# Deformable-convolution layer of a four-layer network: borders of its row tables written earlier, input restored in four pieces, bilinear samples summed two at a time in PSUM

## The reference

```python
# layer 0, position bias of its attention: a small MLP on every (query, key) offset
bias = sign(pos) * log1p(abs(pos))
bias = relu(bias @ cpb_w1 + cpb_b1)
bias = relu(bias @ cpb_w2 + cpb_b2)
bias = bias @ cpb_w3 + cpb_b3
# layer 1
d = conv1x1(depthwise3x3(x[:, :256]));  d = instance_norm(d)
off = conv3x3(d)                          # 18 offsets for each pixel
samples = bilinear(d, grid + off)         # 9 taps, 4 corners, weights (1-ly)(1-lx) ...
dc = einsum('bckhw,ock->bohw', samples, dc_w) + dc_b
dc = layer_norm_over_channels(dc)
das = d * sigmoid(dc)
g = sigmoid(dsc2(max(x[:, 256:])) + dsc2(mean(x[:, 256:])))
x = x * das + x * g
```

## Time and profile before

| | us |
|---|---|
| median of 3 runs | 4365.64 (4363.87 to 4365.74) |
| the profiled execution | 4366.62 |
| its span in the profile | 4364.8 |
| position bias, about | 156 to 2300 |
| layer 1, about | 2803 to 3519 |
| of it, first gather to last sample | 2952.6 to 3498.8 |

### The profile page before, as it was taken

One profiled execution on the slowest core, in us unless ns is written; L12 is line 12 of the kernel. 1 busy time (PEld: TensorE's weight loads), 2 busy tenths in 40 slices (PEclk: granted clock), 3 DMA queues, 4 the chain that ended last, 5 costly groups with the idle time before them and its releaser, 6 DMA issues. The chain is left out here.

```text
span 4364.8 us, 67125 instructions
## 1 busy us (share of the span) xinstructions
PE 3896.5 (89%) x18472; PEld 2384.1 (55%) x18472; DVE 2992.5 (69%) x4467; ACT 2579.8 (59%) x4583; POOL 2118.7 (49%) x1861
## 2 busy tenths in 40 slices
PE   2699999999999999999998999788888377969999
PEld 1455555555555555555556777547666242435553
DVE  7788888888888888888886333447888833235562
ACT  3599999999999999999994333222121330113331
POOL 1555555555555555555551555306667500026663
PEclk7799999999999999999999999889999677989999
DMA  1200000000000000000002000219999911353311
GB/s 45 98 9 11 10 9 9 11 10 9 11 9 9 9 11 10 9 10 10 10 9 81 0 0 0 69 51 350 371 387 376 341 46 60 137 140 69 69 40 77
DMA packets 146902, 326.59 MB, mean 75 GB/s; under 512 B 45737, under 2 KB 46761, under 8 KB 145789
## 3 DMA queue, kind: packets, MB, share of 16 engines
q1 hardware_dynamic: 105340, 174.46, 12.9%
q0 software_dynamic: 41472, 151.01, 8.9%
HBM read 246.14 MB, written 79.04 MB: 74 GB/s over the span
## 5 line engine op out<-in xcount | busy, mean ns | idle before, releaser
L502 POOL TENSOR_TENSOR cpb_sum<-cpb_tab 128x512 f32<-128x512 f32 x1028 | 1045.9, 1048 | 965.7 <-DVE cpb_r L632 965.4
L613 ACT ACTIVATE cpb_h<-cpb_z,net_vec 128x512 f32<-128x512 f32 x1536 | 1006.1, 697 | 50.7 <-PE cpb_z L553 38.2
L550 PE MATMUL cpb_z<-cpb_r,cpb_w2a 128*128 128x512 f32 x2048 | 858.6, 419 | 23.5 <-DVE cpb_h L673 23.5
L632 DVE SCALAR_TENSOR_TENSOR cpb_r<-cpb_sum,cpb_r 128x512 fp32r<-128x512 f32 x1024 | 695.4, 710 | 187.8 <-ACT cpb_r L607 187.8
L551 PE MATMUL cpb_z<-cpb_r,cpb_w2b 128*128 128x512 f32 x2048 | 801.3, 391 | 0.0
L553 PE MATMUL cpb_z<-cpb_r,cpb_w2a 128*128 128x512 f32 x2048 | 799.8, 391 | 0.0
L632 DVE SCALAR_TENSOR_TENSOR cpb_r<-cpb_z,cpb_r 128x512 fp32r<-128x512 f32 x1028 | 661.8, 685 | 160.3 <-ACT cpb_r L607 154.6
L607 ACT ACTIVATE cpb_r<-cpb_z 128x512 fp32r<-128x512 f32 x1028 | 560.4, 604 | 139.5 <-PE cpb_z L537 139.5
L607 ACT ACTIVATE cpb_r<-cpb_sum 128x512 fp32r<-128x512 f32 x1024 | 598.5, 648 | 2.0 <-POOL cpb_sum L502 2.0
L550 PEld LDWEIGHTS cpb_z<-cpb_r,cpb_w2a 128*128 128x128 f32 x2048 | 384.0, 187 | 365.9 <-issue 301.0
L1480 DVE SCALAR_TENSOR_TENSOR dc_acc<-dc_g,dc_wt,dc_acc 128x512 f32<-128x512 f32 x560 | 444.3, 799 | 57.8 <-DMA dc_g<-conv_out,dc_idx 42.0
(11 more groups left out here) (336 smaller groups left out, 5243.2 us busy)
## 6 DMA issues: line engine op xcount, KB each, us to landing
conv_out<-dc_ys SPq DMA_DIRECT2D x576, 64.0 KB, 6.5
cpb_log<-log_dram SPq DMA_DIRECT2D x66, 256.0 KB, 3.1
qk_parts<-gn_r SPq DMA_DIRECT2D x64, 256.0 KB, 2.0
dc_wr<-in_dc_wT SPq DMA_DIRECT2D x9, 1024.0 KB, 5.9
bias_dram<-cpb_bst SPq DMA_DIRECT2D x520, 8.0 KB
net_x<-in_x SPq DMA_DIRECT2D x8, 1024.0 KB, 10.1
sa_qa<-qk_parts SPq DMA_DIRECT2D x16, 512.0 KB
sa_ka<-qk_parts SPq DMA_DIRECT2D x16, 512.0 KB
```

The source lines that it names most:

```text
L502: pool.tensor_tensor(SUM[:, r, :].rearrange("p (y x) -> p y x", x=W), TAB[:, slot, r, 0, :].unsqueeze(1).broadcast_to([P, NF // W, W]), TA ...
L550: pe.matmul(z2[:, bank, :], W2A[:], R1[:, k, :], start=True, stop=False)
L613: act.activation(H2[:, t % 8, :], z2[:, t % 3, :], ACT.Relu, bias=V("cpb_b2")).then_inc(h2a, 1)
L632: v.scalar_tensor_tensor(R2[:, t % RING, :], first_layer(t), 0.0, R1[:, t % RING, :].bitcast(F32), ALU.max, ALU.subtract).then_inc(r2_read ...
```

## The change

1. **Borders.** The six tables are declared in `build`. ZERO and the 18 border DMAs move from SP's list in `layer1` to ACT's list in `layer0_bias`, between its four first parts and its loop; POOL fills ZERO there. SP waits for them at the end of that block. In `layer1` nothing waits for borders any more, and POOL clears only the rims of `dc_dp` instead of the whole tile.
2. **x back in four pieces** of 1 MB: the first after PE's last tile, the others after units 129, 136 and 140 are sampled. `output(n, 0)` waits for its own piece.
3. **Two units in turn.** `sample_two` issues corner k of unit u, then corner k of unit u+1. For units below 120 the running sum of the first three corners is in a PSUM bank (`pn`), and the fourth writes `dc_acc`.
4. The products with the gates move by a unit or two to fit the pairs.

```diff
@@ layer0_bias, POOL and ACT
+            pool.memset(ZERO[:], 0.0).then_inc(blank, 1)
             pool.memset(W3W[:], 0.0).then_inc(win_zero, 1)
...
             act.sem_inc(h2a, FREE)
+            act.wait_ge(blank, 1)
+            HP = H + 4
+            edge, gaps = 2 * HP + 2, H - 1
+            for rows in itertools.chain(*g["conv_out"]):
+                act.dma_start(rows[0:edge, :], ZERO[0:edge, :]).then_inc(borders, 16)
+                act.dma_start(rows[HP * HP - edge:, :], ZERO[0:edge, :]).then_inc(borders, 16)
+                middle = rows[edge + W:edge + W + gaps * HP, :].rearrange("(y x) c -> y x c", x=HP)[:, 0:4, :]
+                act.dma_start(middle, ZERO[0:gaps, :].unsqueeze(1).broadcast_to([gaps, 4, C])).then_inc(borders, 16)
             with act.Fori(0, ITERS) as i:
@@ layer1, SP (the same 18 DMAs leave here)
-            sp.dma_start(X[:].rearrange("p t n -> p (t n)"), x_spill).then_inc(x_back, 16)
-            sp.wait_ge(borders, 16 * 3 * SLOTS * B)
+            for n, units in enumerate((0, LAST[1] + 1, LAST[2] - 4, LAST[3] - 4)):
+                cols = slice(n * NF, (n + 1) * NF)
+                if units:
+                    sp.wait_ge(sampled, units)
+                sp.dma_start(X[:, :, cols], x_spill.rearrange("p (t n) -> p t n", t=CT)[:, :, cols]).then_inc(x_back[n], 16)
@@ layer1, DVE
+            def sample_two(u, tap, b, c):
+                for k in range(4):
+                    for w in (u, u + 1):
+                        n, q = b * 2 + c // 4, (c + w - u) % 4
+                        col = (n * TAPS + tap) * 4 + q
+                        o = ACC[:, n * 4 + q, :]
+                        held = pn[:, w % 4, :] if w < HELD else o
+                        so_far = held if k else DCB[:] if tap == 0 else o
+                        if k:
+                            v.wait_ge(part, u * 3 + (k - 1) * 2 + w - u + 1)
+                        else:
+                            v.wait_ge(gathered[w % GR], 32 * (w // GR + 1))
+                        v.scalar_tensor_tensor(o if k == 3 else held, G[:, w % GR, k // 2, (k % 2) * C:(k % 2 + 1) * C],
+                                               WT[:, k, col:col + 1], so_far, ALU.mult, ALU.add
+                                               ).then_inc(part if k < 3 else sampled, 1)
```

More of the change, by code:

```diff
@@ L1 @@
 from contextlib import ExitStack
+import itertools
 import math
@@ L404, in layer0_bias @@
         LOG, TAB = s.sb("log", [P, 2, 4, 2, W]), s.sb("tab", [P, 2, 4, 2, W])
+        ZERO = s.sb("zero", [P, C])
         H2 = s.sb("h2", [P, 8, NF])
@@ L417, in layer0_bias @@
         log_in, table_step, tables, sum_ready = s.sem("log_in"), s.sem("table_step"), s.sem("tables"), s.sem("sum_ready")
+        blank, borders = s.sem("blank"), s.sem("borders")
         staged = s.sem("bias_staged")
@@ L491, in _ @@
             sp.wait_ge(log_in, 16 * (ITERS + 2))
+            sp.wait_ge(borders, 16 * 18)
             g["prefetch_done"](sp)
@@ L1046, in layer1 @@
         GA = s.sb("ga", [P, CT, B, 2])
-        ZERO, DCB = s.sb("zero", [P, C]), s.sb("dcb", [P, C])
+        DCB = s.sb("dcb", [P, C])
         LM, LR, LN = (s.sb("lm", [P, NT, 4, 2]), s.sb("lr", [P, NT, 4]), s.sb("ln", [P, NT, 4]))
@@ L1053, in layer1 @@
         x_spill = nc.dram_tensor("x_spill", (P, CT * TOK), F32).ap()
-        table = [[nc.dram_tensor(f"conv_out{u}{b}", (HP * HP, C), F32).ap() for b in range(B)] for u in range(SLOTS)]
+        table = g["conv_out"]
         ORDER = [(tap, b) for tap in range(TAPS - 2) for b in range(B)] + [(tap, b) for b in range(B)
@@ L1073, in layer1 @@
                                                               s.sem("gate"))
-        borders, idx_ready = s.sem("borders"), s.sem("idx_ready")
+        idx_ready = s.sem("idx_ready")
         wh_ready, wl_ready = s.sem("wh_ready"), s.sem("wl_ready")
@@ L1082, in layer1 @@
         n_mm, sig, d_whole, gated, x_back, x_ready = (s.sem("n_mm"), s.sem("sig"), s.sem("d_whole"), s.sem("gated"),
-                                                      s.sem("x_back"), s.sem("x_ready"))
+                                                      [s.sem(f"x_back{n}") for n in range(NT)], s.sem("x_ready"))
         block = s.block()
@@ L1111, in _ @@
                 sp.dma_start(OFW[:, k, :, 0:18], d["off_wT"].rearrange("t (k p) o -> k p t o", p=P)[k]).then_inc(w_in, 16)
-            edge = 2 * HP + 2
-            gaps = H - 1
-            for u in range(SLOTS):
-                for b in range(B):
-                    rows = table[u][b]
-                    sp.dma_start(rows[0:edge, :], ZERO[0:edge, :]).then_inc(borders, 16)
-                    sp.dma_start(rows[HP * HP - edge:, :], ZERO[0:edge, :]).then_inc(borders, 16)
-                    middle = rows[edge + W:edge + W + gaps * HP, :].rearrange("(y x) c -> y x c", x=HP)[:, 0:4, :]
-                    sp.dma_start(middle, ZERO[0:gaps, :].unsqueeze(1).broadcast_to([gaps, 4, C])).then_inc(borders, 16)
             weights(1)
@@ L1143, in _ @@
             pool.memset(XP[:, :, 1:H + 1, 0:W + 2:W + 1], 0.0).then_inc(edged, 1)
-            pool.memset(DP[:], 0.0).then_inc(zeroed, 1)
+            images = DP[:].rearrange("p m b h w -> p (m b) h w")
+            pool.memset(images[:, :, 1:H + 3:H + 1, 1:W + 3], 0.0).then_inc(zeroed, 1)
+            pool.memset(images[:, :, 2:H + 2, 1:W + 3:W + 1], 0.0).then_inc(zeroed, 1)
             pool.memset(OFW[:], 0.0).then_inc(zeroed, 1)
-            pool.memset(ZERO[:], 0.0).then_inc(zeroed, 1)
             def weights_low(tap):
@@ L1158, in _ @@
             pool.wait_ge(gate_mm, 1)
-            pool.wait_ge(borders, 16 * 3 * SLOTS * B)
             for i, (tap, b) in enumerate(ORDER):
@@ L1469, in _ @@
             v.wait_ge(dcb_in, 16)
-            def sample(u, tap, b, c):
-                n, q = b * 2 + c // 4, c % 4
-                col = (n * TAPS + tap) * 4 + q
-                o = ACC[:, n * 4 + q, :]
-                v.wait_ge(gathered[u % GR], 32 * (u // GR + 1))
-                for k in range(4):
-                    if k:
-                        v.wait_ge(part, u * 3 + k)
-                    v.scalar_tensor_tensor(o, G[:, u % GR, k // 2, (k % 2) * C:(k % 2 + 1) * C], WT[:, k, col:col + 1],
-                                           DCB[:] if tap == 0 and k == 0 else o, ALU.mult, ALU.add
-                                           ).then_inc(part if k < 3 else sampled, 1)
+            def sample_two(u, tap, b, c):
+                for k in range(4):
+                    for w in (u, u + 1):
[11 more added lines that the diff above has]
+                                               ).then_inc(part if k < 3 else sampled, 1)
             def shifts(n):
@@ L1499, in output @@
                 cols = slice(n * NF, (n + 1) * NF)
-                if n == 0 and m == 0:
-                    v.wait_ge(x_back, 16)
+                if m == 0:
+                    v.wait_ge(x_back[n], 16)
                     v.wait_ge(gate, 1)
@@ L1507, in _ @@
             for i, (tap, b) in enumerate(ORDER):
-                for c in range(CHUNKS):
-                    sample(i * CHUNKS + c, tap, b, c)
+                for c in range(0, CHUNKS, 2):
+                    sample_two(i * CHUNKS + c, tap, b, c)
                     if (i, c) == (len(ORDER) - 3, 6):
@@ L2389, in build @@
             g["prefetch"], g["prefetch_done"] = prefetch, lambda sp: sp.wait_ge(pre, 16 * (CT + 2))
+            g["conv_out"] = [[nc.dram_tensor(f"conv_out{u}{b}", ((H + 4) * (H + 4), C), F32).ap() for b in range(B)]
+                             for u in range(3)]
             layer0_bias(nc, d, g)
```

22 lines of the change are left out of this document (14 added, 8 removed).

## The result

The changed kernel takes **4495.92 us** (median of 4 runs, 4489.74 to 4513.17) against 4364.76 (4363.24 to 4365.74) before: a ratio of 1.0308, 95% interval 1.0286 to 1.0331. It is slower, by 131 us, where the prediction said 82 (4447, range 4350 to 4492). The profiled execution took 4492.03 us, its span is 4490.2, so 125.4 us more than the profiled execution before.

What follows compares the result with a forecast made beforehand. The position bias was taken as PE-bound, layer 1's sampling as near both transfer and DVE limits. 4366.6 + 85 - 16 + 25 - 13 = 4447.6, with the median 1.0 lower: 4447 us, range 4350 to 4492.

Steps and rivals of the forecast that it cites:

- borders on ScalarE in the bias: Position bias: the 18 border DMAs hold ACT about 93 us, part hidden by its idle time; +85 us (68 to 103).
- start of layer 1: Layer 1's first taps: without borders ahead, weights(1) is issued some 19 us earlier; -16 us (-14 to -18).
- pair in a ring of four: Layer 1's sampling: slots come free two at a time, 3.3 to 3.4 us a unit against 3.04; +25 us (-40 to +45).
- x in pieces, end: End of layer 1's sampling: x in four pieces shortens DVE's 9.44 us wait; -13 us (0 to -20).
- the bounds of 76 and 111: Position bias: low and high ends, in us, of the time the 18 border DMAs hold ACT; 93 was taken.
- The smaller memsets end earlier than anyone asks for them: 0: Layer 1's start: POOL clearing only the rims of dc_dp was forecast to change nothing, 0 us.
- T + 4: Sampling ring: fourth gather's start after a pair ends at T; DVE waits until T + 8.5 to 9, four units end T + 13.2 to 13.7.
- the free phase's 3.04: Layer 1's sampling while no tiles are stored: 3.04 us a unit, DVE the limit; base for the pair's loss.
- While tiles are stored the 3.49 is a transfer limit: Layer 1's sampling during stores: a unit's 3.49 us read as transfer-limited; only 0.2 us added there for the pair.
- both cases without that: Rivals with ACT not held by the 18 border DMAs: 4362 us (chance 0.12), or 4310 with faster sampling (0.09).
- Sampling faster by GpSimd's relief: Rival, layer 1: POOL's gathers go out faster, ring no loss, -40 us; 4395 with ACT held (0.17), 4310 not held (0.09).
- Spacing 0.79: Rival, layer 1's sampling: DVE's spacing stays 0.79 us, a pair takes 6.3 us, +32 on the forecast, 4479; chance 0.05.

## Why the prediction was right and wrong

| term | forecast, us | shown |
|---|---|---|
| borders on ScalarE in the bias | +85 (68 to 103) | +98.1 |
| start of layer 1 | -16 (-14 to -18) | -25.8 (borders -16.2, clearing -9.6) |
| pair in a ring of four | +25 (-40 to +45) | +76 alone in the kernel before, +63 against single units in the changed one |
| x in pieces, end | -13 (0 to -20) | -14 with pairs, -5 with single units |
| sum | +81 | +131 (medians); the four above make +134 |

**The hold of ScalarE: right, 13 us short.** That issues queue up behind DMAs carried by one or two engines was read from SyncE's rows and holds on ScalarE's queue. The size was taken between the bounds of 76 and 111; 107.09 was measured. The upper bound's reason, that the prefetch runs at the same time, fits the rows: the first nine issues take 55.2 us on ScalarE and 34.8 on SyncE, the last nine 52.9 and 51.1. That it was the prefetch was not tried.

**Layer 1's start: the borders' term was right, the clearing's was not.** Without the borders the first gather comes 16.2 us sooner, as forecast. The sentence that failed is "The smaller memsets end earlier than anyone asks for them: 0". The memset's end is not what counts; while it runs it holds another engine. It is worth 8.6 us by the run that undid it alone. It is only seen with the borders gone, and so was not to be had from the wait of 24.85 us.

**The pair: the step that failed is the landing.** This term is what put the time outside the range: +25 was forecast, +76 was measured. The burst, the wait for the second unit and the spacing came as forecast. The prediction put the fourth gather's start at T + 4 and its landing "4.5 us (the least) to 7.2 us later", and then went on with T + 8.5 to 9, that is with the least of all landings in the trace of before. After a burst of four it is not the typical one, nor even the least: 5.3 us is the least over the pairs, 7.1 the median. In the rows above, with the release just before 3209.49, the second unit starts 11.4 us after the first gather's start, and 7.2 us after the last one's: the other end of my own range. 16.3 us for four units, not 13.2 to 13.7. Had I taken the 7.2, the turn would have been 11.2 + 4.7 = 15.9 us, 3.98 a unit. The base was wrong as well: I counted from the free phase's 3.04, but over the stage before a unit took 534.3 / 144 = 3.71 us. 144 x (3.98 - 3.71) is +39, and the measured 589.1 / 144 = 4.09 is the +55 of the profiled executions, x pieces included; without them it is 77 (611 less 534.3). What lies between 39 and 77 was not taken apart. One part that shows: GpSimd's waits for stored tiles, the one before the first gather left out, rise from 10.1 us to 27.5.

**A reading that was wrong without harm to the sign.** "While tiles are stored the 3.49 is a transfer limit". As a reading of the stage that was too strong. With single units and six slots the median unit up to unit 125 takes 3.04 us, where it took 3.48 before, and the stage 487 us / 144 = 3.38 on average at 402 GB/s. The number alone does not tell the cause: from 2980 to 3002, at a share of 1.04, units take 3.5 us with six slots too. The DMA share of 0.96 over the stage was high and was no proof: one that is at its end shows 1.03 to 1.04 here without a break. Since I took the stage for transfer-bound, I gave the pair 0.2 us there and not 0.6.

**The rivals.** ScalarE was held, so both cases without that fell. Sampling faster by GpSimd's relief: the relief came, and the run of single units in PSUM against the one in SBUF shows it by itself (median gather instruction 1.19 to 0.94 us), but it had nothing to speed up while no slot was free. It agrees with the rule of the Trainium skill ("SBUF — State Buffer", "Who interferes with whom") that the prediction cited. Spacing 0.79: it was 0.66. Spacing that stays at 0.79 was to be 4479, close to the measured time, but not by what happened. The range ended at 4492, 4 us short: it held the ring's worst case at +45 where the pair costs +76. That the miss of the range is only 4 us is luck, since the clearing's 9.6 us went the other way.

## What to carry to other kernels

Count a ring in slots on their way, not in slots: work that takes two at a time and gives both back at its end leaves a ring of four with bursts and gaps (4.09 us a unit instead of 3.71); add a slot, or give each part back as soon as it is read, before making the vector work faster. Before moving a DMA to an idle queue look at its shape: here slowest dimensions of 70, 80 and 32 instead of 74 and 31, with some rows more, made the issues nearly free (11.7 us instead of 108), and then their place did not matter. Where a step's price is a latency, take the latency under the load that the change itself makes; the minimum of all is not it.

## What the runs showed of the hardware

- A write of 74 rows or 31 gaps held the issuing engine up to 19.89 us, and 18 of them 108 us; 18 of 70, 80 and 32 took 11.7 us. On both queues the first three of the 18 went at once and the fourth was held. The Trainium skill ("DMA: Bandwidth & Descriptors", "Why a DMA increments its semaphore by 16 and not by 1") gives the number of engines; that the issuing engine pays for it is what the rows add.
- A GpSimd memset of 128x10368 took 8.76 us, and a VectorE operation that took 2.51 us beside short memsets took 10.20 beside it (9.73 and 2.50 in the pair of runs that differ in it alone).
- VectorE's operations with the sum in PSUM take as long as in SBUF (medians 756 and 752 ns in single units); chained ones are spaced 0.79 us in both, two chains in turn 0.66.
- The most that the transfers of this stage reached in 40 us was 414 GB/s, at a DMA share of 1.04. With six slots the median landing of a gather was 9.9 us and more, with four and single units 8.0.
